# Flamingo block on one core: weight loads spread over the first rows, keys' low parts made once, one wait in each turn

## What is computed

```python
x = x + tanh(g_xattn) * attention(layernorm(x), ctx, ctx, mask)   # 8 batches, 224 rows, 32 heads of 64,
                                                                  # 8 key/value heads, 750 context rows
# attention: scores = q k^T / 8 + mask; softmax over 750; times v (k and v are both the context)
x = x + tanh(g_ffn) * ffn(layernorm(x))
# ffn: router over 512 slots, top 8, softmax, aux values, down and up projection,
#      gated by an uncertainty that has a 2048 -> 512 gelu layer (w1) and a query projection (wq)
```

## Time and profile before

| | |
|---|---|
| median of 3 runs | 1129.11 us (1128.87 to 1129.16) |
| the profiled execution | 1128.4 us, span 1126.6 us |
| granted TensorE clock, mean | 0.997 |
| busy: TensorE, ScalarE, VectorE, GpSimd | 1068.5, 890.6, 862.4, 864.7 us |
| attention stage | up to about 826 us of the span |

### The profile page before, as it was taken

The page is one execution under the profiler, slowest core; times in us unless marked ns, Lnnn a source line. Parts: engine busy times, 40 slices in busy tenths (PEclk is TensorE's granted clock), DMA queues, the critical chain, the costliest instruction groups (busy, mean ns, idle before and its releaser), DMA issues.

```text
span 1126.6 us, 42864 instructions
## 1 busy us (share of the span) xinstructions
PE 1068.5 (95%) x18241; PEld 773.3 (69%) x18276; DVE 862.4 (77%) x2134; ACT 890.6 (79%) x1159; POOL 864.7 (77%) x600
## 2 busy tenths in 40 slices
PE   4899999899999999999999999999979999999998
PEld 2777777677777777777777777777757565555554
DVE  4777777788778878877887788788844899666776
ACT  3899998899899999999999999999941454555544
POOL 4889999999999999999999999999950111414324
PEclk9999999999999999999999999999999999999999
DMA  9423222232222323232232222122136300011224
GB/s 317 132 59 78 81 59 72 72 90 69 74 82 67 71 72 83 72 92 82 58 79 73 82 72 66 44 59 72 31 144 219 144 1 1 1 76 75 113 89 173
DMA packets 102589, 95.57 MB, mean 85 GB/s; under 512 B 84481, under 2 KB 85505, under 8 KB 98562
## 3 DMA queue, kind: packets, MB, share of 16 engines
q1 hardware_dynamic: 101682, 91.79, 27.7%
q10 hardware_dynamic: 720, 1.05, 0.3%
HBM read 71.75 MB, written 20.97 MB: 82 GB/s over the span
## 4 chain that ended last, share of the span: by engine, by line
PE 63%; POOL 18%; issue 8%; ACT 6%; DVE 2%; DMA 1%; SPq 1%; POOLq 0%; DVEq 0%; ACTq 0%
PE psum L954 13%; PE psum L1010 12%; PE psum L941 12%; POOL arena L592 11%; PE psum L986 6%; PE psum L974 5%; PE psum L975 4%; ACT arena L753 3%; PE psum L1096 3%; ACT arena L757 2%; POOL arena L550 2%; PE psum L997 2%; POOL arena L619 1%; PE psum L921 1%; POOL arena L557 1%
## 5 line engine op out<-in xcount | busy, mean ns | idle before, releaser
L592 POOL TENSOR_TENSOR arena<-arena 128x1536 bf16<-128x1536 f32 x224 | 615.4, 2750 | 27.5 <-ACT arena L753 27.1
L1366 DVE CUSTOM_DVE_ANT_0 arena<-psum,arena 128x750 f32<-128x750 f32 x448 | 405.8, 937 | 129.7 <-PE psum L941 110.4
L757 ACT ACTIVATE arena<-arena,neg_max 128x750 f32<-128x750 f32 x448 | 409.6, 914 | 4.4 <-DVE neg_max L1366 4.4
L753 ACT ACTIVATE arena<-psum 128x768 f32<-128x768 f32 x448 | 363.3, 811 | 58.1 <-PE psum L954 42.9
L954 PE MATMUL psum<-ident,arena 64*128 64x64 f32 x5376 | 265.1, 230 | 30.5 <-ACT arena L753 25.4
L954 PEld LDWEIGHTS psum<-ident,arena 64*128 64x128 f32 x5376 | 210.1, 139 | 104.0 <-issue 89.7
L941 PE MATMUL psum<-arena 64*128 64x512 bf16 (+1 forms) x2688 | 259.4, 324 | 3.8 <-DVE neg_max L1366 2.2
L975 PE MATMUL psum<-arena 128*128 128x64 bf16 (+1 forms) x2688 | 198.8, 193 | 1.4 <-issue 1.4
L974 PE MATMUL psum<-arena 128*128 128x65 bf16 (+1 forms) x2688 | 199.3, 195 | 0.0
L941 PEld LDWEIGHTS psum<-arena 64*128 64x128 bf16 x2688 | 123.6, 95 | 92.2 <-issue 6.3
L975 PEld LDWEIGHTS psum<-arena 128*128 128x128 bf16 (+1 forms) x2688 | 177.1, 98 | 1.5 <-issue 1.5
(11 more groups left out here) (167 smaller groups left out, 1081.3 us busy)
## 6 DMA issues: line engine op xcount, KB each, us to landing
arena<-in_k_t SPq DMA_DIRECT2D x128, 187.5 KB, 3.2
arena<-in_v_rows SPq DMA_DIRECT2D x64, 192.0 KB, 3.4
out<-arena SPq DMA_DIRECT2D x10, 1024.0 KB, 3.9
arena<-in_x_top SPq DMA_DIRECT2D x8, 1024.0 KB, 6.4
arena<-in_x_rest SPq DMA_DIRECT2D x8, 768.0 KB, 5.3
spill<-arena SPq DMA_DIRECT2D x96, 64.0 KB, 2.2
arena<-spill SPq DMA_DIRECT2D x6, 1024.0 KB, 10.7
arena<-in_w_t SPq DMA_DIRECT2D x4, 1024.0 KB, 13.8
```

What stands on the lines that cost most here:

```text
L592: pool.tensor_tensor(p_lo[:, slots, :], p_sb[:, slots, :], high(p_sb[:, slots, :]), ALU.subtract).then_inc(p_split, 1)
L753: act.activation(p_sb[:, n % RING, :].rearrange("p (c h q) -> p h c q", h=2, q=HALF), turned_ps, ACT.Copy).then_inc(evac_a, 1)
L757: act.activation(s_sb[:, n % RING, 0:CTX], s_sb[:, n % RING, 0:CTX], ACT.Exp, bias=neg_max[:, n % 4, :], scale=-1.0).then_inc(exped, 1)
L1366: dve.tensor_tensor_reduce(s_sb[:, n % RING, 0:CTX], flat_ps[:, score_at(s):score_at(s) + CTX], mask_sb[:, max(m - REP + 1, 0), :], -1.0, ...
```

## The change

1. **One wait in each turn.** `turn_unit(n)` waits for the copy of unit n-1 alone. ScalarE's order has the exponential of unit n ahead of that copy.
2. **Keys' low parts made once.** From group 3 on (`APART`), a group's keys are loaded a second time as 128x375 (first half of the columns in partitions 0 to 63, second half in 64 to 127) into `k_apart`; GpSimd makes the low part of that, and SyncE copies it into both halves of `k_lo` with four DMAs of 64x375. The split of a group comes two or three steps of the loop earlier or later than before: group 2 at i = 1, the odd group at p = 2, the next even group at p = 4. The scores wait for keys and moves only at p = 0 and p = 3.
3. **Weight loads spread.** The small tables are loaded in pair 0, w1's quarters in pairs 1, 2, 3 and 5, wq in pair 6. w1's low parts are made one in each pair from 3 to 18 (p = 6), wq's in pair 20, and ScalarE rounds wq in pair 8 instead of pair 1.

```diff
+APART = 3
-        carve("attention", [128, 188])
+        k_apart_lo = carve("attention", [128, 376], BF16)
+        k_apart = carve("attention", [128, CTX // 2])
+        def moves(g):
+            return 64 * ((g - APART) // 2 + 1)
+            def load_k_apart(g):
+                if g > APART:
+                    sp.wait_ge(k_split, g)
+                for part in range(2):
+                    cols = slice(CTX // 2 * part, CTX // 2 * part + CTX // 2)
+                    sp.dma_start(k_apart[D * part:D * part + D, :], k_t[g][:, cols]).then_inc(k_apart_loaded, 16)
+            def move_k_lo(g):
+                sp.wait_ge(k_split, g + 1)
+                for part in range(2):
+                    cols = slice(CTX // 2 * part, CTX // 2 * part + CTX // 2)
+                    for s in range(2):
+                        sp.dma_start(k_lo[D * s:D * s + D, g % 2, cols],
+                                     k_apart_lo[D * part:D * part + D, 0:CTX // 2]).then_inc(k_lo_moved[g % 2], 16)
...
-            load_v(2)
             load_top(1)
             load_rest(1)
-            for i in range(4):
+            load_v(2)
+            load_k_apart(APART)
...
                     load_k(2 * both + 2)
+                    if 2 * both + 2 >= APART:
+                        move_k_lo(2 * both + 2)
+                        load_k_apart(2 * both + 3)
...
                     load_k(2 * both + 3)
+                    move_k_lo(2 * both + 3)
+                    if both + 2 < PAIRS:
+                        load_k_apart(2 * both + 4)
                     sp.wait_ge(valued, 2 * UNITS * both + UNITS)
                     load_v(2 * both + 3)
+                if both == 0:
+                    load_small()
+                if both in (1, 2, 3, 5):
+                    load_w1((1, 2, 3, 5).index(both))
+                if both == 6:
+                    sp.dma_start(wq_raw, wq_t).then_inc(weights_loaded, 16)
...
+                pool.wait_ge(k_apart_loaded, 32 * (g - APART + 1))
+                if g > APART:
+                    pool.wait_ge(k_lo_moved[(g - 1) % 2], moves(g - 1))
+                pool.tensor_tensor(k_apart_lo[:, 0:CTX // 2], k_apart[:, :], high(k_apart[:, :]), ALU.subtract).then_inc(k_split, 1)
...
+                if i == 1:
+                    split_k(2)
-                    if p == 1:
-                        split_k(2 * both + 2)
-                    if p == 4:
+                    if p == 2:
                         split_k(2 * both + 3)
+                    if p == 4 and both + 2 < PAIRS:
+                        split_k(2 * both + 4)
-                if p in (2, 6) and 2 <= both < 2 + KC // 2:
-                    n = 2 * (both - 2) + p // 6
+                if p == 6 and 3 <= both < 3 + KC:
+                    n = both - 3
-                if p in (2, 6) and both == 10:
+                if p in (1, 6) and both == 20:
-                if both == 1 and p == 3:
+                if both == 8 and p == 3:
...
-                pe.wait_ge(k_split, groups[1] + 1)
+                if p in (0, 3):
+                    g = groups[1]
+                    if g < APART:
+                        pe.wait_ge(k_split, g + 1)
+                    else:
+                        pe.wait_ge(k_loaded[g % 2], 32 * (g // 2 + 1))
+                        pe.wait_ge(k_lo_moved[g % 2], moves(g))
...
             def turn_unit(n):
-                pe.wait_ge(exped, n + 1)
                 if n == 0:
+                    pe.wait_ge(exped, 1)
                     pe.wait_ge(pads_zero, 1)
-                if n >= 1:
+                else:
                     pe.wait_ge(evac_a, n)
```

More of the change, by code:

```diff
@@ L242, in flamingo_block @@
         v_loaded = [sem(f"v_loaded{i}") for i in range(3)]
+        k_apart_loaded = sem("k_apart_loaded")
         k_split = sem("k_split")
+        k_lo_moved = [sem("k_lo_moved0"), sem("k_lo_moved1")]
         v_split = sem("v_split")
@@ L426, in _, with load_small, load_w1 @@
             load_v(1)
-            load_v(2)
             load_top(1)
             load_rest(1)
-            for i in range(4):
-                sp.dma_start(w1_raw[:, 4 * i:4 * i + 4, :], w1_t[i]).then_inc(w1_loaded[i], 16)
[L432 to L436, removed]
+            load_v(2)
+            load_k_apart(APART)
+            def load_small():
+                for dst, src in ((wr_t[:, :], wr), (wr_rows[:, :], wr_rows_in), (scal, scalars), (keys_raw[0:BOT, :], keys_t), (keys_raw[BOT:128, :], keys_t)):
+                    sp.dma_start(dst[:], src).then_inc(small_loaded, 16)
+                sp.wait_ge(pads_set, 1)
+                sp.dma_start(rk_aug[BOT:BOT + 1, :], log_rel).then_inc(rel_loaded, 16)
+            def load_w1(i):
+                sp.dma_start(w1_raw[:, 4 * i:4 * i + 4, :], w1_t[i]).then_inc(w1_loaded[i], 16)
             for both in range(PAIRS):
@@ L546, in split_k @@
             def split_k(g):
[L547 to L551, removed]
+                if g < APART:
+                    pool.wait_ge(k_loaded[g % 2], 32 * (g // 2 + 1))
+                    if g >= 2:
+                        pool.wait_ge(scored, UNITS * (g - 1) + (g + 1) % 2)
+                    pool.tensor_tensor(k_lo[:, g % 2, :], k_raw[:, g % 2, :], high(k_raw[:, g % 2, :]), ALU.subtract).then_inc(k_split, 1)
+                    return
+                pool.wait_ge(k_apart_loaded, 32 * (g - APART + 1))
+                if g > APART:
+                    pool.wait_ge(k_lo_moved[(g - 1) % 2], moves(g - 1))
+                pool.tensor_tensor(k_apart_lo[:, 0:CTX // 2], k_apart[:, :], high(k_apart[:, :]), ALU.subtract).then_inc(k_split, 1)
             def split_v(g):
```

## The result

| | kernel before | changed kernel |
|---|---|---|
| median (range) | 1128.99 us (1126.84 to 1129.16) | **1101.73 us** (1099.06 to 1102.88) |
| profiled execution, span | 1128.4, 1126.6 us | 1101.9, 1100.0 us |
| 29 pairs, 2 to 30 | 728.66 us | 709.26 us |
| pair 0 | 29.45 us | 25.22 us |

The ratio is **0.9759, 95% interval 0.9738 to 0.9781**: faster by 27 us, where 22.5 were forecast and the range ended at 1104.0. The time is outside the range, on the good side. The sign is right, and the sum is wrong in two of its terms, in opposite directions.

What follows compares the result with a forecast made beforehand. GpSimd was taken to bound the early attention pairs, then a ring of TensorE turns and ScalarE copies. Terms 10.4 + 8.9 - 0.4 + 3.6 = 22.5 us off 1128.4 gave 1105.9, median 1106.6 us; range 1104 to 1117.5.

Steps and rivals of the forecast that it cites:

- 173 steps x 0.060 = 10.4 us: Attention loop: one wait per turn saves 0.060 us at each odd turn, in 173 steps, 10.4 us in all.
- 0.113 to 0.053: Odd turns: the gap from ScalarE's copy end to TensorE's first weight load shrinks from 0.113 to 0.053 us.
- 3.81 us of unbroken ScalarE work: Steps where ScalarE also normalises: ScalarE is already the limit at 3.81 us, so one wait gains nothing there.
- 8.9 us less, 0.4 back: Attention pairs: lighter, spread GpSimd work removes its 8.9 us excess over undisturbed pairs; backlog in four pairs returns 0.4.
- it is even; between 0 and 1 us of waiting: Split at p = 4: half-size keys land at 357.3 us, GpSimd arrives at 357.5; it waits 0 to 1 us.
- It has room: GpSimd in attention pairs: 23.0 us of work against TensorE's 24.1 us pair, so it can absorb the load's wait.
- 3.6 us less: Pair 0: the keys' load no longer queues behind the weights, saving 3.6 us, bounds 3.2 to 3.6.
- B: Odd turns: the copy's wait costs the same in a weight load, so one wait gains nothing; 1117.0 us, chance 0.12.
- C: GpSimd's half-size keys' load lands late; at 1.7 us late each of 29 pairs loses 0.5, 1121 us; chance 0.08.
- D: Moves of the keys' low parts land late and hold TensorE 2 us in each of 29 pairs; 1165 us, chance 0.04.
- E: Even turns gain too: 0.06 us of the 0.16 us gap ahead goes, another 10 us, 1096 us; chance 0.06.
- the steps of 3.30 us: Sign in the attention loop: plain steps fall from 3.36 to 3.30 us.

Runs made afterwards that it cites:

- two_waits_again: The changed kernel with the wait on the exponential put back in every turn; 1117.28 us, 0.9895 of the kernel before.
- even_turns_two: The changed kernel with the second wait put back in the even turns alone; 1103.01 us, 0.9782 of the kernel before.
- late_split: The changed kernel with the half-size keys' split moved from p = 4 to 6 and the first weights' slice from 6 to 4; 1096.58 us.

## Why the prediction was wrong, step by step

**Part 1, "173 steps x 0.060 = 10.4 us": mis-sized by a factor of two, twice over.** Measured are 18.1 us in pairs 2 to 30 (719.8 - 701.7), and 0.6 in each of pairs 0, 1 and 31: **19.9 us**.

- *The size.* 0.113 to 0.053 was forecast for the gap, and 0.113 to 0.051 came. The other 0.03 us is turn b itself (0.549 to 0.519). Its load group takes 0.46 us where the earlier trace rows has 0.48 and turn a has 0.45. With the wait in the load, the turn runs like turn a, the second load of each two 0.003 us behind the first and not 0.03. I had the row, 0.48 against 0.45, and asked nothing of it. That the loads behind a waiting load are already queued, and those behind a semaphore instruction are not, would explain it; no run separates this.
- *The count.* I gave nothing to the steps with a normalising step on ScalarE, "3.81 us of unbroken ScalarE work". Here is the kernel before, ScalarE in such a step (the last two are in the earlier trace rows):

```profile
407.92 0.81 ACT L753 ACTIVATE arena<-psum 128x768 f32<-128x768 f32 x1 [0.16 <-PE psum L954]
408.62 0.92 ACT L757 ACTIVATE arena<-arena,neg_max 128x750 f32<-128x750 f32 x1
409.50 0.81 ACT L753 ACTIVATE arena<-psum 128x768 f32<-128x768 f32 x1
410.21 0.91 ACT L757 ACTIVATE arena<-arena,neg_max 128x750 f32<-128x750 f32 x1
```

From an exponential's start to the next copy's it is 0.88 us (408.62 to 409.50), from the same exponential to L728 0.81 (410.21 to 411.02).
**Parts 2 and 3, "8.9 us less, 0.4 back": 2.0 us came.** The excess went from 8.9 to 6.9 (7.6 less ScalarE's 0.7). The failing step is the race at p = 4, "it is even; between 0 and 1 us of waiting". By the terms of that sum, for the 18 late loads: from the start of SyncE's block (the issue of the keys' two loads, 431.29 in the rows above) to the end of the half-size loads' issue 5.9 us (forecast 4.8). In the mean the keys' two loads take 1.1 of it (1.1), the wait for the odd split 0.56 (0.2), the four moves 2.7 (2.3) and the two half-size loads 1.5 (1.2). Most issues take 0.60 us where 0.56 was assumed, and single ones up to 2 us. Then it is 2.1 us more in the median until the split starts (the forecast's landing, counted from the issue's end, is 2.6). GpSimd asks 7.44 us after the block's start, where the forecast left it at the old 7.55. "It has room" failed as well, where a weight slice follows: GpSimd waits 1.5 us, and pair 17 pays 0.65; without a slice (pairs 24 and 25) it had the room. At the old pace the term nearly held: 8.9 - 1.3 = 7.6 us came of 8.9 - 0.4 = 8.5, leaving out the 0.7 of pair 8 (`two_waits_again`: 2.0 - 0.7 = 1.3 of excess).

**Part 4, "3.6 us less": right.** Pair 0 went from 29.45 to 25.81 us with two waits in the turns: 3.64, with the new keys' splits in it too.

**Sum in the profiles**: 19.9 + 2.0 + 3.6 = 25.5, with 0.8 after the last copy and 0.2 ahead of the first that I don't explain: 26.5, and the spans differ by 26.6.

**The rivals.** B is refuted in the form given: the weight load took up the wait in 0.051 us. C came in its mild form: the late load cost some 5 us, but the time stayed below the forecast, since part 1 gave 9.5 us more than its term. D did not come: TensorE shows no wait for a move, in any pair. E is refuted by `even_turns_two`: the 0.154 us stay whatever stands there. What the prediction told from the Trainium skill (TensorEngine Tiling (Array Packing), Key Properties), that changing the tiling mode drains TensorE, agrees with this; that the 0.154 us are this drain, no run shows by itself.

**The range** fell short since its low end took every step as gaining 0.06 us and no more. That the time came out near it at all owes something to two misses that partly cancel, 9.5 us too little for part 1 and 6.5 too much for parts 2 and 3. Of the signs listed, the gap, the missing instruction and pair 0 came; the steps of 3.30 us did not (3.27), and a sign of being wrong did, a wait for the new load of over 1 us (up to 1.8). GpSimd's 38 us of 40 came nearly:

```profile
120.00:160.00 40.00, 38.98 (x824) 29.94 (x822) 31.86 (x85) 36.35 (x48) 38.18 (x21) 1.00 0.49 138
440.00:480.00 40.00, 39.17 (x827) 29.98 (x821) 32.64 (x89) 36.65 (x48) 38.66 (x21) 1.00 0.40 99
```

Beside the earlier trace rows the second line already shows the loss: TensorE, which bounds this stretch, went from 39.77 to 39.17 us of 40. In `late_split` it is busy 39.98 there.

## What to carry to other kernels

Let the instruction itself carry the wait that ends last, and a separate semaphore instruction the one that is met early: here the order of two lines was worth 0.09 us in every step that nothing else held. Before calling an engine's round a floor, compare the start-to-start time of the same instruction ahead of different followers; the smallest is its own, the rest is a wait that no bracket shows. When several edits meet, redo each race between engines at the new pace: here two pieces of GpSimd's work, swapped, gained 5 us more.

## What the runs showed of the hardware

- A wait that ends last costs 0.051 us from the producer's end to the weight load when the load carries it, 0.113 us when a semaphore instruction of 51 ns does, and the group of 12 loads behind it is 0.03 us longer, since the second load of each two starts 0.03 us after the first and not 0.003. The same instruction costs nothing when its wait was met before.
- Moves from SBUF to SBUF of 64 rows of 750 bytes (46.9 KB) land 2.4 us after issue in the median, but each takes some 0.60 us of SyncE's queue (0.5 to 1.9), and the half-size load stands behind four of them, 2.7 us in the mean for the late ones:

```profile
arena<-arena SPq DMA_DIRECT2D x244, 46.9 KB, 2.4
```
